# A layer kernel with its loops written out, each tile loaded a turn earlier, and a new list of steps

## The chip, the cores and the metric

The kernel runs on one core of a Trainium2 chip. The metric is the device time of one execution in microseconds. PE is the matmul engine, PEld its weight loads, DVE and ACT the vector and the scalar engine, POOL and SP the two others; SP issues all DMAs here.

## The reference

Four graph layers, each with a residual and a layer norm, over 128 graphs of 64 nodes and 512 features:

```
x = layernorm(x + hypergraph(x, adj, W1, W2))        # layer 0
x = layernorm(x + pairwise(x, adj, w, a))            # layer 1
h = relu(adj @ (x @ W1) + b1)                        # layer 2
h = relu(adj @ (h @ W2) + b2)
x = layernorm(x + adj @ (h @ W3) + b3)
q, k, v = split(x @ W_qkv)                           # layer 3, 8 heads of 64
attn = 0.33 softmax(q k^T / 8) + 0.33 adj + 0.33 exp(-adj)
x = layernorm(x + (attn @ v) @ W_out + b_out)
```

## The kernel before

Two graphs of 64 nodes make a tile of 128 rows; there are 64 tiles, worked on four at a time (tiles 0 to 3 of a turn), so 16 turns. The program has two halves, one after the other with a barrier between: `hypergraph_and_pairwise` does layers 0 and 1 and stores x2 to memory, `convolutions_and_attention` reads x2 and does layers 2 and 3.

In each half every engine goes through one hand-written list, ORDER, and does its own part of each entry: `g0.1` is step g0 of tile 1, and a `+` says that it belongs to the next turn (software pipelining). START holds the entries with `+` (turn 0), then a hardware loop (Fori) runs ORDER 15 times, and END holds the entries without `+`. In the loop, the values that a wait compares with are computed in registers at the head of each turn. The engines meet only through semaphores. SP has a loop of its own with the loads and the stores.

The steps of the second half, with their lines: `at` turns the adjacency blocks AB into AT (DVE, line 1024). `t0`, `t1`, `t2` multiply by the adjacency: 32 small matmuls of 64 x 64 (PE 1140), a cast of the result to Th (ACT 942) and the remainder Tl (DVE 1004). `g0`, `g1`, `g2` are projections of 12 matmuls of 128 x 512 (PE 1109); behind g0 and g1 DVE adds the bias (1032) and ACT does the relu (946). `b3` adds a bias to X (1035), `z3`, `rs3`, `x3` are residual and norm (DVE 1042, 1007 to 1011, POOL 864, DVE 1047), `xp` transposes (PE 1150), `v` and `qk` project (PE 1109; qk for a pair of tiles, 96 matmuls of 256 columns; its copies to QK on ACT 962 and DVE 1054), `s` makes scores (PE 1171, DVE 1058 to 1062), `sm` the softmax (ACT 966, DVE 1065 to 1073), `ta` transposes it (PE 1178, copies ACT 971 and DVE 1076), `av` multiplies by v (PE 1185, ACT 974, DVE 1004), `wo` projects, `z4`, `rs4`, `x4` are the last residual and norm (DVE 1084, POOL 864, DVE 1089), `cm` prepares masks (ACT 951, POOL 869 to 881). In the first half `tx`, `t2`, `t3` are small matmuls (PE 581), `y1`, `y2`, `y3` projections (PE 561).

Before, PE's part of the second list reads: ta.0 ta.1 av.0 s.2 s.3 av.1 wo.0 wo.1 ta.2 t0.0+ av.2 g0.0+ wo.2 ta.3 t0.1+ av.3 t1.0+ g0.1+ wo.3 t0.2+ t1.1+ ... xp.2+ qk.0+ xp.3+ v.2+ v.3+ s.0+ s.1+ qk.1+, and then the jump back.

X holds the residual of a tile until `z4`; SP loads the next tile into it behind `z4` (line 808), and `t0` waits for that load.

Of the kernel before, what the change touches and what calls it, by code (L numbers as in the profile page):

```python
# [44 lines left out]
def hypergraph_and_pairwise(nc, semaphores, x, adj, W1T, b1, gamma, beta, W2T, b2, w, wT, a, x2, slots, later):  # L45
# [9 lines left out]
    with ExitStack() as ctx:  # L55
# [162 lines left out]
        def _(pool):  # L218
# [60 lines left out]
            with pool.Fori(0, iters - 1) as it:  # L279
                steps(ORDER, it, pool.to_reg)  # L280
# [3 lines left out]
        def _(act):  # L284
# [80 lines left out]
            with act.Fori(0, iters - 1) as it:  # L365
                steps(ORDER, it, act.to_reg)
# [3 lines left out]
        def _(dve):  # L370
# [174 lines left out]
            with dve.Fori(0, iters - 1) as it:  # L545
                steps(ORDER, it, dve.to_reg)
# [3 lines left out]
        def _(pe):  # L550
# [122 lines left out]
            with pe.Fori(0, iters - 1) as it:  # L673
                steps(ORDER, it, pe.to_reg)
# [11 lines left out]
def convolutions_and_attention(nc, semaphores, x2, adj, mask_rows, mask_cols, E, AA, QK, slots, b1, b2, b3, Wqkv, bout, out):  # L686
# [9 lines left out]
    with ExitStack() as ctx:  # L696
# [23 lines left out]
        X = sb("X2", [P, CH, D])  # L720
        H = sb("H", [P, CH, D])
# [14 lines left out]

        def by_graph(W, c):
            return W[:, :, c * P:(c + 1) * P].rearrange("p k (g j) -> p k g j", g=2)
# [4 lines left out]
        blocks_in = sem("blocks_in")  # L743
# [6 lines left out]
        (at_ok, mc_ok, row_ok, mm_ok, bs_ok, exp_adj, bt3, cm2, cm_ok, b3_ok, bo_ok, z3, bn3, mv3,  # L750
         ve3, rs3, x3_ok, xp_ps, xph, xp_sb, v_ps, v_sb, s_ps, sbs_ok, max_ok, nb_ok, ex_ok, rec_ok, rla_ok, soft_ok, attn_ok,
         ta_psA, ta_psB, ta_sbA, ta_sbB, av_ps, avh, av_sb, wo_ps, z4, bn4, mv4, ve4, rs4, x4_ok) = map(sem, (
            "at_ok2 mc_ok row_ok mm_ok bs_ok exp_adj bt3 cm2 cm_ok b3_ok bo_ok z3 bn3_2 mv3_2 "
# [31 lines left out]
        def _(sp):  # L785
            def load_blocks(tile):

                for g in range(2):
                    for b in range(2):
                        for c in range(CH):  # L790
                            sp.dma_start(AB[g * C + b * C // 2:g * C + (b + 1) * C // 2, c, :].rearrange("p (a j) -> p a j", a=2),
                                         adj_b[g, b, :, bass.ds(tile + c, 1), :, :].rearrange("i t a j -> i (t a) j")).then_inc(blocks_in, 16)
# [14 lines left out]
            def load_x(c, tile):  # L807
                sp.dma_start(X[:, c, :], x2[bass.ds(tile, 1)].rearrange("a r d -> (a r) d")).then_inc(x_in[c], 16)
# [4 lines left out]
            load_blocks(0)  # L813
            for c in range(CH):
                load_x(c, c)
            load_masks(0)
            for k in range(KD):
                sp.wait_ge(split_lo, (4, 4, 6, 8)[k])
                sp.dma_start(raw_qkv[k], Wqkv[k * P:(k + 1) * P, :]).then_inc(load_in[k], 16)
            for i in range(2):  # L820
# [21 lines left out]
            sp.wait_ge(blocks_in, 16 * 4 * CH * iters)  # L842
# [5 lines left out]
        def _(pool):  # L848
# [48 lines left out]
            with pool.Fori(0, iters - 1) as it:  # L897
                steps(ORDER, it, pool.to_reg)
# [33 lines left out]
        def _(act):  # L932
            def steps(entries, it, reg):
# [3 lines left out]
                for step, c, ahead in entries:  # L937
# [9 lines left out]
                    if step == "cm":  # L947
                        act.wait_ge(masks_in, loaded[ahead])
                        if entries is not START:
                            act.wait_ge(attn_ok, at[ahead - 1][CH - 1])  # L950
# [31 lines left out]
            with act.Fori(0, iters - 1) as it:  # L982
                steps(ORDER, it, act.to_reg)
# [259 lines left out]
```

## Time and profile before

| | |
|---|---|
| median of 3 runs | 2844.67 us (2843.2 to 2847.39) |
| the profiled execution | 2846.66 us, span 2844.9 us |
| busy: PE | 2659.1 us, 93% |
| busy: PEld | 2197.8 us, 77% |
| busy: DVE | 1820.5 us, 64% |
| busy: ACT | 879.0 us, 31% |
| busy: POOL | 474.9 us, 17% |
| mean granted clock of TensorE | 0.978 |

The first half ends near 1158 us, the second half's weights are ready near 1194 us, its loop runs from 1279 to 2811 us. A busy share is a mean over stages. "Issue" in the profile is time in which an engine waited for nothing that the profile shows. Busy times of matmuls overlap, so the distance from one start to the next says more of their cost than their durations.

### The profile page before, as it was taken

The numbers are of one execution on the slowest core, as the hardware profiler recorded it, in microseconds if no ns is written. First come the engines' busy times: TensorE is split into PE (matmuls) and PEld (weight loads), VectorE is DVE, ScalarE is ACT, GpSimd is POOL, SyncE is SP. The second block draws the span as 40 slices with busy tenths as digits, with TensorE's granted clock in tenths as the row PEclk, the third lists the DMA queues.
The fourth block names the chain that finished last, engine by engine and source line by source line (L and its number), as shares of the span: only waits on it lengthen the run. The fifth ranks groups of instructions, "written<-read, shape, count | busy, mean of one in ns | idle before, by whom it ended". The sixth has DMA issues, their size and how long they took to land.

```text
span 2844.9 us, 73879 instructions
## 1 busy us (share of the span) xinstructions
PE 2659.1 (93%) x30296; PEld 2197.8 (77%) x30296; DVE 1820.5 (64%) x3754; ACT 879.0 (31%) x2397; POOL 474.9 (17%) x749
## 2 busy tenths in 40 slices
PE   3999999999999999299999999999999999999998
PEld 2778778777777778287788788788788778878877
DVE  3778887788878887446545655654654655565565
ACT  2222322222222222233332332333333333233233
POOL 0222222222222222010110111011011011101101
PEclk9999999999999999699999999999999999999999
DMA  5111111111111110201101100100110110110010
GB/s 181 28 38 36 35 35 35 38 36 36 38 36 40 42 35 19 97 6 33 37 8 33 38 13 28 36 25 19 33 31 13 33 38 10 29 38 17 26 32 16
DMA packets 130004, 99.41 MB, mean 35 GB/s; under 512 B 89104, under 2 KB 91152, under 8 KB 129808
## 3 DMA queue, kind: packets, MB, share of 16 engines
q1 hardware_dynamic: 129808, 96.30, 11.4%
q8 instruction: 184, 3.01, 0.5%
q14 instruction: 12, 0.10, 0.0%
HBM read 62.68 MB, written 33.55 MB: 34 GB/s over the span
## 4 chain that ended last, share of the span: by engine, by line
PE 52%; DVE 4%; issue 2%; ACT 1%; SPq 1%; DMA 0%; DVEq 0%; POOLq 0%
PE qs L1109 43%; PE qs L1140 4%; PE qs L1171 1%; PE qs L1178 1%; DVE T2l L1004 1%; PE qs L1150 1%; PE qs L1185 1%; ACT T2h L942 1%; DVE sm L1007 0%; DVE Z L1084 0%; DVE E L1069 0%; DVE E L1073 0%; DMA QK<-in_L_Wqkv 0%; DVE sm L1060 0%; DVE E L1058 0%
## 5 line engine op out<-in xcount | busy, mean ns | idle before, releaser
L1109 PE MATMUL qs<-hi,T2h 128*128 128x512 f32 x1024 | 422.0, 412 | 24.5 <-DVE T2l L1004 24.1
L1109 PE MATMUL qs<-hi,T2l 128*128 128x512 f32 x1024 | 406.9, 397 | 0.0
L1109 PE MATMUL qs<-lo,T2h 128*128 128x512 f32 x1024 | 406.5, 397 | 0.0
L1004 DVE TENSOR_TENSOR T2l<-qs,T2h 128x512 fp32r<-128x512 f32 x320 | 212.9, 687 | 183.1 <-ACT T2h L942 110.9
L864 POOL TENSOR_TENSOR sm<-sm,mhalf 128x1 f32<-128x1 f32 x128 | 86.2, 673 | 1370.6 <-DVE sm L1011 1370.6
L1109 PE MATMUL qs<-T2h,WQh 128*128 128x256 f32 x1024 | 291.2, 284 | 0.0
L1109 PE MATMUL qs<-T2h,WQl 128*128 128x256 f32 x1024 | 288.2, 281 | 0.0
L1109 PE MATMUL qs<-T2l,WQh 128*128 128x256 f32 x1024 | 288.1, 281 | 0.0
L1109 PEld LDWEIGHTS qs<-hi,T2h 128*128 128x128 f32 x1024 | 194.6, 190 | 78.5 <-DVE T2l L1004 34.8
L1109 PEld LDWEIGHTS qs<-hi,T2l 128*128 128x128 f32 x1024 | 194.5, 190 | 46.1
L1109 PEld LDWEIGHTS qs<-lo,T2h 128*128 128x128 f32 x1024 | 195.1, 190 | 39.8
L561 PE MATMUL ps<-W2h,Th 128*128 128x512 f32 x512 | 204.3, 399 | 5.1 <-issue 4.5
L561 PE MATMUL ps<-W1h,Th 128*128 128x512 f32 x512 | 206.8, 404 | 0.6 <-DVE Tl L411 0.6
L561 PE MATMUL ps<-W1l,Th 128*128 128x512 f32 x512 | 201.4, 393 | 0.0
L561 PE MATMUL ps<-W1h,Tl 128*128 128x512 f32 x512 | 201.2, 393 | 0.0
L561 PE MATMUL ps<-W2h,Tl 128*128 128x512 f32 x512 | 199.7, 390 | 0.0
L561 PE MATMUL ps<-W2l,Th 128*128 128x512 f32 x512 | 199.5, 390 | 0.0
L946 ACT ACTIVATE H<-H 128x512 f32<-128x512 f32 x128 | 81.2, 634 | 368.5 <-DVE H L1032 368.5
L1109 PEld LDWEIGHTS qs<-T2h,WQh 128*128 128x128 f32 x1024 | 192.7, 188 | 1.1
L1109 PEld LDWEIGHTS qs<-T2l,WQh 128*128 128x128 f32 x1024 | 192.8, 188 | 0.0
L1109 PEld LDWEIGHTS qs<-T2h,WQl 128*128 128x128 f32 x1024 | 192.7, 188 | 0.0
L966 ACT ACTIVATE E<-E,sm 128x64 f32<-128x64 f32 x512 | 172.0, 340 | 32.1 <-DVE sm L1062 31.6
(175 smaller groups left out, 5319.3 us busy)
## 6 DMA issues: line engine op xcount, KB each, us to landing
X<-in_x SPq DMA_DIRECT2D x64, 256.0 KB, 6.5
x<-R SPq DMA_DIRECT2D x64, 256.0 KB, 2.0
X<-x SPq DMA_DIRECT2D x64, 256.0 KB, 2.9
out<-Z SPq DMA_DIRECT2D x64, 256.0 KB, 3.1
AB<-in_adj SPq DMA_DIRECT2D x512, 8.0 KB, 1.6
A<-in_adj SPq DMA_DIRECT2D x128, 32.0 KB, 2.2
An<-in_adj SPq DMA_DIRECT2D x16, 128.0 KB, 2.3
WB<-in_adj SPq DMA_DIRECT2D x32, 64.0 KB, 7.3
```

Of the source, the lines that this page charges most:

```text
L561: mm = pe.matmul(out, lhsT, rhs, start=start and i == 0, stop=i == len(terms) - 1)
L864: return pool.tensor_tensor(col(c, RS), col(c, VE), mhalf[:, :], ALU.pow)
L942: act.copy(by_graph(Th, c), halves(c)).then_inc(th[i], 1)
L946: act.activation(H[:, c, :], H[:, c, :], ACT.Relu).then_inc(g_sb[i], 1)
L966: last = act.activation(EH(c)[:, h, :], EH(c)[:, h, :], ACT.Exp, bias=col(c, NB + h), scale=SCALE, accum_out=col(c, SUM + h))
L1004: return dve.tensor_tensor(lo, ps, hi.bitcast(F32), ALU.subtract)
L1109: mm = pe.matmul(out, lhsT, rhs, start=i == 0, stop=i == len(terms) - 1)
L1140: mm = pe.matmul(half[q, k * C:(k + 1) * C], rows[g, k * P + q.start:k * P + q.stop], AT[g, c, :], start=True, stop=True)
L1150: mm = pe.transpose(psA[c][:, k * P:(k + 1) * P], X[:, c, k * P:(k + 1) * P], ident[:, :])
L1171: mm = pe.matmul(ps[c][y * C:(y + 1) * C, x, (n_ * 2 + g) * C:(n_ * 2 + g + 1) * C], QK[x * C:(x + 1) * C, m, rows_g], QK[x * C:(x + 1) * ...
L1178: mm = pe.transpose(ps[c][:, x, n_ * P:(n_ + 1) * P], E[:, c, x * 2 + n_, :], ident[:, :])
L1185: mm = pe.matmul(ps[c][x * C:(x + 1) * C, g, (2 * n_ + y) * C:(2 * n_ + y + 1) * C], H[rows_g, c, h * DHEAD:(h + 1) * DHEAD], AA[rows_g, c ...
```

## The change

In both halves the loops of PE, DVE, ACT and POOL become Python loops, so that the 15 turns stand written out in a row, with numbers in place of registers. SP keeps its loops. In the second half:

- Tile c of the next turn is loaded into a buffer of its own, `xn(c)`: XN for tiles 0 and 1, an unused part of AA for 2 and 3. The load waits for the two readers of that buffer, `t0.c` (PE) and `b3.c` (DVE), and no longer for `z4.c`. `t0` reads xn(c); it now waits for `z4` of the tile before itself, since both use the same PSUM banks. `b3` reads xn(c) and writes X.
- AB is turned into AT in two instructions, for tiles 0 and 1 (`at.0`) and 2 and 3 (`at.1`), each with its own semaphores; the blocks are loaded per pair.
- The stores come behind all loads of SP's turn.
- ORDER is new. PE's part reads: s.1 qk.1 ta.0 ta.1 s.2 av.0 av.1 s.3 wo.0 wo.1 ta.2 t0.0+ av.2 g0.0+ t0.1+ wo.2 ta.3 t1.0+ av.3 g0.1+ wo.3 t0.2+ t1.1+ g1.0+ g1.1+ t2.0+ t0.3+ ... g2.2+ t2.3+ v.1+ xp.2+ g2.3+ qk.0+ xp.3+ v.2+ v.3+ s.0+.

```diff
+        XN = sb("XN", [P, 2, D])
+        def xn(c):
+            return XN[:, c, :] if c < 2 else AA[:, 3 - c, HEADS // 2:HEADS, :].rearrange("p h j -> p (h j)")
...
         ORDER = order(
-            "ta.0 ta.1 av.0 s.2 s.3 av.1 wo.0 z4.0 sm.2 wo.1 rs4.0 x4.0 at.0+ ta.2 t0.0+ av.2 b3.0+ z4.1 sm.3 rs4.1 g0.0+ "
-            "wo.2 x4.1 ta.3 t0.1+ av.3 z4.2 b3.1+ t1.0+ rs4.2 g0.1+ wo.3 x4.2 t0.2+ t1.1+ z4.3 rs4.3 x4.3 g1.0+ b3.2+ g1.1+ "
-            "t0.3+ t2.0+ g0.2+ g2.0+ z3.0+ rs3.0+ b3.3+ t1.2+ t2.1+ g0.3+ x3.0+ g1.2+ xp.0+ g2.1+ z3.1+ rs3.1+ bo.0+ t1.3+ "
-            "t2.2+ x3.1+ v.0+ g1.3+ xp.1+ g2.2+ bo.1+ t2.3+ z3.2+ v.1+ rs3.2+ x3.2+ g2.3+ z3.3+ rs3.3+ x3.3+ xp.2+ bo.2+ "
-            "qk.0+ cm.0+ xp.3+ bo.3+ v.2+ v.3+ s.0+ s.1+ sm.0+ sm.1+ qk.1+")
+            "s.1 sm.0 bo.2 bo.3 sm.1 qk.1 ta.0 ta.1 s.2 av.0 av.1 rs4.0 s.3 sm.2 z4.0 wo.0 at.0+ wo.1 ta.2 rs4.1 x4.0 t0.0+ "
+            "av.2 z4.1 sm.3 g0.0+ rs4.2 rs4.3 b3.0+ x4.1 t0.1+ wo.2 ta.3 at.1+ t1.0+ av.3 z4.2 g0.1+ x4.2 wo.3 z4.3 t0.2+ "
+            "t1.1+ g1.0+ x4.3 g1.1+ b3.1+ t2.0+ rs3.0+ b3.2+ t0.3+ b3.3+ g0.2+ g2.0+ z3.0+ t1.2+ t2.1+ x3.0+ rs3.1+ g0.3+ "
+            "g1.2+ xp.0+ g2.1+ z3.1+ t2.2+ t1.3+ v.0+ x3.1+ g1.3+ xp.1+ rs3.2+ g2.2+ z3.2+ t2.3+ x3.2+ v.1+ xp.2+ bo.0+ z3.3+ "
+            "g2.3+ x3.3+ qk.0+ bo.1+ rs3.3+ xp.3+ v.2+ cm.0+ v.3+ s.0+")
...
@@ SP, second half @@
             with sp.Fori(0, iters - 1) as it:
                 t0 = sp.snap(it * CH)
-                sp.wait_ge(at_ok, sp.snap(it + 1))
-                load_blocks(t0 + CH)
+                for p in range(2):
+                    for c in (2 * p, 2 * p + 1):
+                        sp.wait_ge(t_ps[0], sp.snap(t0 + (c + 1)))
+                        sp.wait_ge(b3_ok, sp.snap(t0 + (c + 1)))
+                        load_x(c, t0 + (CH + c))
+                    sp.wait_ge(at_ok[p], sp.snap(it + 1))
+                    load_blocks(t0 + CH, p)
                 sp.wait_ge(cm_ok, sp.snap(it + 1))
                 load_masks(t0 + CH)
                 for c in range(CH):
-                    sp.wait_ge(z4, sp.snap(t0 + (c + 1)))
-                    load_x(c, t0 + (CH + c))
-                    if c:
-                        store(c - 1, t0)
-                store(CH - 1, t0)
+                    store(c, t0)
...
@@ PE, second half; the same in the other engines and in the first half @@
             steps(START, -1, number)
-            with pe.Fori(0, iters - 1) as it:
-                steps(ORDER, it, pe.to_reg)
+            for it in range(iters - 1):
+                steps(ORDER, it, number)
             steps(END, iters - 1, number)
...
@@ DVE @@
-                        dve.transpose(AT[:, :, :].rearrange("p c i -> p (c i)"), AB[:, :, :].rearrange("p c i -> p (c i)")).then_inc(at_ok, 1)
+                        pair_c = slice(2 * c, 2 * c + 2)
+                        alone(blocks_in[c], blocks[ahead])
+                        if each[ahead] > 1:
+                            dve.wait_ge(t_ps[2], (each[ahead] - 2) * CH + 2 * c + 2)
+                        dve.transpose(AT[:, pair_c, :].rearrange("p c i -> p (c i)"), AB[:, pair_c, :].rearrange("p c i -> p (c i)"))\
+                            .then_inc(at_ok[c], 1)
...
-                        dve.wait_ge(t_ps[0], n[c])
-                        dve.tensor_tensor(X[:, c, :], X[:, c, :], b3_all[:, :], ALU.add).then_inc(b3_ok, 1)
+                        dve.wait_ge(x_in[c], x_loaded[ahead])
+                        dve.tensor_tensor(X[:, c, :], xn(c), b3_all[:, :], ALU.add).then_inc(b3_ok, 1)
...
@@ PE, step t0 @@
-                            alone(at_ok, each[ahead])
+                            alone(at_ok[c // 2], each[ahead])
                             pe.wait_ge(x_in[c], x_loaded[ahead])
+                            if n[c] > CH:
+                                pe.wait_ge(z4, n[c] - CH)
```

## Rows read from the trace of the kernel before

**Rows 1.** The page: code fetches (packets, MB, share); groups (busy, mean ns, idle before).

```profile
q8 instruction: 184, 3.01, 0.5%
...
L1004 DVE TENSOR_TENSOR T2l<-qs,T2h 128x512 fp32r<-128x512 f32 x320 | 212.9, 687 | 183.1 <-ACT T2h L942 110.9
...
L966 ACT ACTIVATE E<-E,sm 128x64 f32<-128x64 f32 x512 | 172.0, 340 | 32.1 <-DVE sm L1062 31.6
```

**Rows 2.** Waits of PE: for whom, us in total, times, longest.

```profile
PE qs L1178 <- issue: 30.1, 14, 2.4
...
PE ps L561 <- issue: 4.5, 14, 0.4
```

**Rows 3.** Lines 1195 and 673, PE's loops: duration ns min/median/max, first and last start.

```profile
L1195 PEldq COMPARE_BRANCH  x15: 79/3619/3799, 1375.5 to 2809.3; - x15
...
L673 PEldq COMPARE_BRANCH  x15: 76/208/245, 169.7 to 1116.3; - x15
```

**Rows 4.** Timeline of PE around a jump: start us, length us, engine, line, idle before.

```profile
1787.78 0.28 PE L1109 MATMUL qs<-T2h,WQl 128*128 128x256 f32 x1
...
1790.28 1.72 PE L1178 MATMUL qs<-ident,E 128*128 128x128 f32 x8 [2.23 <-issue]
...
1795.02 0.51 PE L1109 MATMUL qs<-hi,T2h 128*128 128x512 f32 x1
...
1801.89 0.66 PE L1178 MATMUL qs<-ident,E 128*128 128x128 f32 x4 [0.66 <-DVE E L1073]
1802.74 0.69 PE L1140 MATMUL qs<-AT,X 64*64 64x64 f32 x32 [0.20 <-issue]
...
1804.86 0.50 PE L1109 MATMUL qs<-hi,T2h 128*128 128x512 f32 x1 [0.95 <-DVE T2l L1004]
...
1818.98 0.69 PE L1140 MATMUL qs<-AT,X 64*64 64x64 f32 x32
```

**Rows 5.** The same view where the loop is left.

```profile
2811.18 0.28 PE L1109 MATMUL qs<-T2h,WQl 128*128 128x256 f32 x1
2811.30 1.03 PE L1178 MATMUL qs<-ident,E 128*128 128x128 f32 x8
...
2815.06 0.50 PE L1109 MATMUL qs<-hi,T2h 128*128 128x512 f32 x1
```

**Rows 6.** Stretches: busy us (count) of PE, PEld, DVE, ACT, POOL; clock, DMA.

```profile
1587.00:1689.00 102.00, 96.59 (x1103) 81.57 (x1102) 57.41 (x113) 33.86 (x106) 11.76 (x14) 1.00 0.10 27
1790.60:1794.00 3.40, 3.40 (x76) 2.94 (x77) 1.10 (x3) 1.33 (x3) 0.00 (x0) 0.50 0.00 0
```

**Rows 7.** Chain that ended last: start us, us; the matmuls of qk.1.

```profile
1776.47 11.59 PE qs L1109 x96
```

**Rows 8.** Timeline of PE, first half, first passes: y2.2 three times, a wait.

```profile
101.64 0.49 PE L561 MATMUL ps<-W2h,Th 128*128 128x512 f32 x1
...
147.57 0.45 PE L581 MATMUL ps<-CU,R 64*64 64x64 f32 x12 [0.66 <-issue]
...
170.43 0.49 PE L561 MATMUL ps<-W2h,Th 128*128 128x512 f32 x1 [0.36 <-issue]
...
238.03 0.49 PE L561 MATMUL ps<-W2h,Th 128*128 128x512 f32 x1 [0.32 <-issue]
```

**Rows 9.** Timeline of DVE, with a cast of ACT, in the stretch of rows 4.

```profile
1793.13 0.59 ACT L974 CAST T2h<-qs 128x512 fp32r<-128x512 f32 x1 [1.15 <-PE qs L1185]
...
1794.36 0.68 DVE L1058 TENSOR_TENSOR E<-qs,BS 128x512 f32<-128x512 f32 x1
...
1795.90 0.69 DVE L1058 TENSOR_TENSOR E<-qs,BS 128x512 f32<-128x512 f32 x1
...
1798.10 0.69 DVE L1084 TENSOR_TENSOR Z<-qs,X 128x512 f32<-128x512 f32 x1
...
1799.98 0.19 DVE L1065 RECIPROCAL sm<-sm 128x8 f32<-128x8 f32 x1
...
1802.20 0.43 DVE L1024 STREAM_TRANSPOSE AT<-AB 128x256 f32<-128x256 f32 x1
```

More of the change, by code:

```diff
@@ L364, in _ @@
             steps(START, -1, number)
-            with act.Fori(0, iters - 1) as it:
-                steps(ORDER, it, act.to_reg)
+            for it in range(iters - 1):
+                steps(ORDER, it, number)
             steps(END, iters - 1, number)
@@ L544, in _ @@
             steps(START, -1, number)
-            with dve.Fori(0, iters - 1) as it:
-                steps(ORDER, it, dve.to_reg)
+            for it in range(iters - 1):
+                steps(ORDER, it, number)
             steps(END, iters - 1, number)
@@ L672, in _ @@
             steps(START, -1, number)
-            with pe.Fori(0, iters - 1) as it:
-                steps(ORDER, it, pe.to_reg)
+            for it in range(iters - 1):
+                steps(ORDER, it, number)
             steps(END, iters - 1, number)
@@ L742, in convolutions_and_attention @@
         load_in = [sem(f"load2_in{i}") for i in range(KD)]
-        blocks_in = sem("blocks_in")
+        blocks_in = [sem(f"blocks_in{p}") for p in range(2)]
+        at_ok = [sem(f"at_ok2_{p}") for p in range(2)]
         masks_in = sem("masks_in")
@@ L812, in _ @@
             sp.wait_ge(consts_ok, 3)
-            load_blocks(0)
-            for c in range(CH):
+            for p in range(2):
+                load_blocks(0, p)
+            for c in range(2):
                 load_x(c, c)
@@ L819, in _ @@
                 sp.dma_start(raw_qkv[k], Wqkv[k * P:(k + 1) * P, :]).then_inc(load_in[k], 16)
+                if k == 2:
+                    load_x(2, 2)
+            sp.wait_ge(split_lo, len(pieces) + KD - 1)
+            load_x(3, 3)
             for i in range(2):
@@ L827, in _ @@
                 t0 = sp.snap(it * CH)
-                sp.wait_ge(at_ok, sp.snap(it + 1))
-                load_blocks(t0 + CH)
+                for p in range(2):
+                    for c in (2 * p, 2 * p + 1):
+                        sp.wait_ge(t_ps[0], sp.snap(t0 + (c + 1)))
[3 more added lines that the diff above has]
+                    load_blocks(t0 + CH, p)
                 sp.wait_ge(cm_ok, sp.snap(it + 1))
@@ L841, in _ @@
                 sp.wait_ge(x_in[c], 16 * iters)
-            sp.wait_ge(blocks_in, 16 * 4 * CH * iters)
+            for p in range(2):
+                sp.wait_ge(blocks_in[p], 16 * 2 * CH * iters)
             sp.wait_ge(masks_in, 16 * MASK_LOADS * iters)
@@ L896, in _ @@
             steps(START, -1, number)
-            with pool.Fori(0, iters - 1) as it:
-                steps(ORDER, it, pool.to_reg)
+            for it in range(iters - 1):
+                steps(ORDER, it, number)
             steps(END, iters - 1, number)
@@ L948, in steps @@
                         act.wait_ge(masks_in, loaded[ahead])
-                        if entries is not START:
-                            act.wait_ge(attn_ok, at[ahead - 1][CH - 1])
+                        if each[ahead] > 1:
+                            act.wait_ge(attn_ok, (each[ahead] - 1) * CH)
                         act.copy(MM[:, :, :, :], mrow[:, :, :, :]).then_inc(row_ok, 1)
@@ L981, in _ @@
             steps(START, -1, number)
-            with act.Fori(0, iters - 1) as it:
-                steps(ORDER, it, act.to_reg)
+            for it in range(iters - 1):
+                steps(ORDER, it, number)
             steps(END, iters - 1, number)
@@ L1016, in steps @@
                 stored = [[reg(it * 32 + (32 * a + 16 * (r + 1))) for r in range(2)] for a in (0, 1)]
-                blocks = [reg(it * (64 * CH) + 64 * CH * (a + 1)) for a in (0, 1)]
+                x_loaded = [reg(it * 16 + 16 * (a + 1)) for a in (0, 1)]
+                blocks = [reg(it * (32 * CH) + 32 * CH * (a + 1)) for a in (0, 1)]
                 for step, c, ahead in entries:
@@ L1092, in _ @@
             steps(START, -1, number)
-            with dve.Fori(0, iters - 1) as it:
-                steps(ORDER, it, dve.to_reg)
+            for it in range(iters - 1):
+                steps(ORDER, it, number)
             steps(END, iters - 1, number)
@@ L1194, in _ @@
             steps(START, -1, number)
-            with pe.Fori(0, iters - 1) as it:
-                steps(ORDER, it, pe.to_reg)
+            for it in range(iters - 1):
+                steps(ORDER, it, number)
             steps(END, iters - 1, number)
```

19 lines of the change are left out of this document (7 added, 12 removed).

## The prediction, made before the changed kernel ran

> **What bounds the kernel now.** I read the profile from the outside in. First the page: PE is busy 93% of the span (the table above), and code is fetched in 184 packets of 3.01 MB in all [rows 1]. So the reader should look only for time in which PE waits, and ask who ends it. The list of PE's waits gives it [rows 2]: 30.1 us in 14 waits "for issue" ahead of line 1178, and only 4.5 us in 14 waits for issue at line 561. Line 1178 is the first PE line of a turn in the second half, line 561 that of the first half, and 14 is the number of jumps back. Third, the branch lines [rows 3]: the taken jump of PE's second loop takes 3619 ns in the median, that of the first loop 208 ns. Both jumps are the same instruction, so what differs is what it jumps into: the long body of the second half has to be brought in again, the body of the first does not.
>
> Fourth, one turn of the second half in order of time [rows 4]. The last matmul of `qk.1` starts at 1787.78, `ta.0` at 1790.28: 2.50 us. Where no jump lies between them, at the end of the loop, the same two starts are 0.12 us apart [rows 5]. So a jump costs 2.38 us here, of which the profile shows 2.23 as idle. Then `ta.0` to `wo.0` takes 4.74 us in the loop and 3.76 us after it [rows 4, 5], for the same matmuls: the idle time drops the granted clock to its lower level (1.2 GHz) in the stretch behind this jump [rows 6]; not behind every jump, for 1587 to 1689 has 1.00 throughout. Further on PE waits 0.66 us for `ta.2` (softmax of tile 2) and 0.95 us for `g0.0` [rows 4]. Ten turns lie between 1790.28 and 2811.30, 102.1 us each [rows 4, 5].
>
> **The change, part by part.**
>
> *1. Jump of the second half, removed 14 times.* The idle part: 30.1 us [rows 2], scaled by 2.38 / 2.23 to starts, 32 us. The slower stretch behind it: 4.74 - 3.76 = 0.98 us, times 14, 14 us. Together -46 us. The register arithmetic that goes with it lies inside the same gap. SP keeps its loop. For DVE, ACT and POOL the jump is not on the path: PE starts `ta.0` later than their own list is ready, and it will still be PE that comes last behind `qk.1`, 11.6 us of matmuls [rows 7].
>
> The Trainium skill ("Advanced Engine Details and Errata", Control Flow Timing) gives a compare-and-branch about 108 ns; by that figure 28 jumps are worth 3 us and, with the list, the forecast would be about 2824. The trace does not agree for either loop, 208 and 3619 ns [rows 3], and leaves this case no chance. The same page (ISA Cache) gives TensorE 128 KB in lines of 16 KB and the other engines 32 KB, and "Vector Engine (DVE) Microarchitecture Reference" (The three layers) 64 bytes an instruction; by these the second body of PE does not fit and the first does, which agrees with the two durations, and it speaks against unrolling the first half, which is part 2.
>
> *2. Jump of the first half, removed 14 times, and its code fetched anew.* Gain: 4.5 us idle [rows 2], about 6 us by starts. Cost: until now only the first pass had to be fetched. It took 170.43 - 101.64 = 68.8 us against 238.03 - 170.43 = 67.6 us, and PE stood idle for issue 0.66 us in the middle of a dense run of small matmuls (`t2.1`) [rows 8]. Written out, every pass is a first pass. Bounds: nothing (the long 128x512 matmuls leave time to fetch, and no wait for issue of size stands inside the second half's body, which is fetched each turn) and 15 x 1.2 = 18 us. Whether a boundary of fetched code falls into the dense run changes from turn to turn; I take a third, 6 us. Net 0, between -6 and +12.
>
> *3. The new list between `qk.1` and `t0.2`, walked.* Units: a cast on ACT 0.59 [rows 9], a remainder on DVE 0.69, eight exponentials of one tile 8 x 0.34 = 2.7 [rows 1]; 96 matmuls of 256 columns take 11.6 [rows 7], so a projection (12 of 512 columns) 2.8 to 2.9; a step of 32 small ones 0.5 (3.76 for four of them, eight transposes and small waits, [rows 5]). Time runs from the last start of `qk.1`, no jump. PE does `ta.0 ta.1 s.2 av.0 av.1 s.3`, the same matmuls as in [rows 5], and is free at 3.5 to 3.9. But on DVE `s.2` now stands ahead of the remainder of `av.0`: scores of tile 2 are there at 2.2, they hold DVE 1.54 us (1794.36 to 1795.90 for one tile [rows 9]), then 0.69 for the remainder: `wo.0` starts at 4.5. That is a new wait of 0.6 to 1.0 us. `wo.0` and `wo.1` end at 10.1. ACT's exponentials of tile 2 begin at 3.9 behind the `av.1` cast and take 2.7; DVE's sm.2 takes 1.9 (1799.98 to the start of `ta.2`, 1801.89 [rows 4, 9]) and now comes before `z4.0`: done at 8.6, so `ta.2` no longer waits (-0.66). `z4.0` with its statistics takes 1.9 to 2.0 (before, from 1798.10, ending behind the first operation of sm.2 [rows 9]), to 10.55; the half-size transposition, some 0.25, comes next, and `t0.0` starts at 10.9, 0.3 after `ta.2`. Cast 0.59 and remainder 0.69 follow: `g0.0` at 12.95, a wait of about 1.0, as before. From there g0.0 2.88, `t0.1` 0.5 (now ahead of `wo.2`, which only the early load allows), wo.2 2.8, `ta.3` 0.5, `t1.0` 0.5, 0.4 for the AA copy of tile 3, which stands on DVE behind `x4.1` and `t0.1`, `av.3` 0.5, g0.1 2.88, wo.3 2.8: `t0.2` at 26.7, 26.6 after `ta.0`. Before it is 1818.98 - 1790.28 = 28.7, and 27.7 without the slow stretch that part 1 has counted. Gain 1.1 us.
>
> *4. The rest of the list.* `xp.2` now follows `g2.2` after only `t2.3` and `v.1` (3.3 us), while z3.2, statistics, POOL's power and x3.2 need about 3.6: a new wait of 0.3. The `cm.0` step comes one projection later; its result reaches DVE's s.0 about 1.4 us late, hidden by `qk.1` (11.6 us, of which scores, exponentials and softmax of tiles 0 and 1 use some 11). If that cover is gone, `ta.0` waits up to 1 us. Net of parts 3 and 4: -0.8 a turn, -12 us; bounds -30 (all new waits vanish) and +15 (each is a microsecond longer).
>
> *5. Early loads and the pair-wise transposition.* `t0.0` (1802.74) follows the AT transposition, which starts at 1802.20 [rows 4, 9], and not the load. So the second buffer is worth nothing itself, only through the list. New waits: on SP x(c) waits for `t0.c` and b3.c, with blocks, masks and stores queued behind; all are needed most of a turn later, except the stores, which need x4 and find SP idle there. On PE `t0.c` waits for z4 of the tile before, done at 9.3 in the walk against 10.9. DVE has one more transposition instruction, and b3 keeps its size. Cost 0, hidden by DVE's idle time.
>
> *6. Start and end.* The list is cut elsewhere: `s.1` and `qk.1` go from the start to the end, equal work. The end has no t0 and g0 between the tiles, and loses the wait for sm.2: -3 us. Two of the turns before are some 2 us longer than the others by a double slow stretch behind the jump: -3 us.
>
> Sum: -46 + 0 - 12 - 3 - 3 = -64 us. The profiled execution took 2846.7 (its span 2844.9 and 1.8 around it), 2.0 above the median of the runs; a difference carries over: 2844.7 - 64 = 2781.
>
> **The rivals.**
> (a) *The list gives nothing*: only the jump is gone, 2845 - 46 = 2799. For it: two waits leave and three come. Against: the longest (`ta.2`) surely goes. Chance 0.17.
> (b) *The new wait at `wo.0` drops the clock* in each turn, as the jump did: +0.98 x 15 = 15, 2796. For it: it follows small matmuls, as in [rows 6]. Against: before, 0.66 and 0.95 us of waiting within 4 us left the clock at 1.00 in the turn from 1587 [rows 4, 6]. Chance 0.12.
> (c) *Waits of the list vanish* since engines run closer than my walk: 2845 - 46 - 30 - 6 = 2763. Chance 0.13.
> (d) *Slower: PE starves for code.* Written out, all 30 turns fetch. It decides from (64 + 6) / 30 = 2.3 us of stall a turn; at 2.5 a turn +75 against -64 gives 2856. The one measured first pass shows 1.2 in all, and the second half fetches each turn without it. (The cache sizes of the page named in part 1 are the rule that speaks for this case.) Chance 0.04. That unrolling costs just what it saves (within 0.2%): 0.03.
> (e) *The change does not do what it says*: loads still land late since x waits for b3. b3.0 to b3.3 stand in the first half of a turn, the use a turn later: excluded.
>
> **How the numbers follow.** Forecast 2781 with chance 0.51, its own range 2770 to 2792. The range reaches to (a), (b) and (c) with the bound of part 2 on top: 2760 to 2808. Faster than 0.2% (about what this kernel's runs can tell from no change): 0.51 + 0.17 + 0.12 + 0.13 = 0.93; same 0.03; slower 0.04.
>
> **What the changed profile would show.** Right: no wait for issue at the turn's first matmul; `ta.0` 0.1 us behind `qk.1`; granted clock 1.00 through the loop; turns of 98.2 us; first-half turns of 67 to 68.5 us with short waits for issue at line 581; code packets up by half or more; at `wo.0` a wait for line 1004 of 0.6 to 1.0. Wrong: waits for issue in the small matmuls of both halves (d), turns of 99 or more with the clock at 1.00 (a), lower clock behind `wo.0` (b).

## The result, and the profile after

| | before | after |
|---|---|---|
| median, us | 2844.13 (2843.2 to 2847.39) | 2779.22 (2776.96 to 2780.73) |
| ratio | | 0.977, 95% interval 0.975 to 0.979 |
| span of the profiled execution | 2844.9 | 2775.1 |
| first starts of the second half's turns | 1278.57 to 2811.30 | 1265.58 to 2733.19 |
| mean turn of the second half | 102.2 | 97.8 |
| mean turn of the first half | 67.7 | 67.6 |

The forecast was 2781, the range 2760 to 2808. By medians the change is worth 64.9 us; the two profiled spans differ by 69.8, since the one of before lies 2.5 us above its median and the one of after 2.3 us below. In the traces the loop of the second half gives 65.1 of it, the first half's loop 0.3, the end 3.8, the start 0.9 (the start differs by up to 3 us between traces of the same code), and the stretch between the two loops takes 0.3 back. A turn of the second half is counted from `ta.0` before and from `s.1` after, the first entry of each list. One further execution of a kernel below, `loop_first`, took 3290.38 us at a mean granted clock of 0.75, and its ratio leaves that one out.

The page of after: span, and the code fetches that answer to [rows 1].

```profile
span 2775.1 us, 73243 instructions
...
q8 instruction: 240, 3.93, 0.6%
```

The waits of PE in after (for whom, us in total, times, longest), against [rows 2]. The 30.1 us for issue are gone, and 14 waits at line 561 with them; what is left for issue is 1.3 us in the first half and 0.2 in the second. The line for T2l, 29.9 us in 35 waits, is two waits in each turn: the one at `wo.0` is new (0.8 us each), the one at `g0.0` stood in the old list too (0.95 in [rows 4], 0.85 now).

```profile
PE qs L1124 <- DVE T2l L1016: 29.9, 35, 1.4
...
PE ps L581 <- issue: 1.3, 2, 0.9
```

The windows view over the whole second half of after, in the columns of [rows 6]: the granted clock is 1.00 all through.

```profile
1199.00:2758.90 1559.90, 1529.58 (x17566) 1299.12 (x17565) 932.07 (x1802) 535.67 (x1685) 162.70 (x221) 1.00 0.09 26
```

The timeline of after where [rows 4] stood, PE and the operations of DVE that set its waits (start us, length us, engine, line, operation, idle before). `ta.0` follows `qk.1` after 0.12 us. `wo.0` (1672.89) waits for the remainders of `av.0` and `av.1` (1672.15), which stand behind the scores of tile 2 (1670.63). `g0.0` (1681.32) waits for the remainder of `t0.0` (1680.57). `t0.2` starts 26.7 us after `ta.0`.

```profile
1668.62 0.28 PE L1124 MATMUL qs<-T2h,WQl 128*128 128x256 f32 x1
1668.74 1.04 PE L1195 MATMUL qs<-ident,E 128*128 128x128 f32 x8
...
1670.63 0.69 DVE L1073 TENSOR_TENSOR E<-qs,BS 128x512 f32<-128x512 f32 x1 [0.33 <-PE qs L1188]
...
1672.15 1.28 DVE L1016 TENSOR_TENSOR T2l<-qs,T2h 128x512 fp32r<-128x512 f32 x2
...
1672.89 0.50 PE L1124 MATMUL qs<-hi,T2h 128*128 128x512 f32 x1 [0.79 <-DVE T2l L1016]
...
1676.85 0.68 DVE L1099 TENSOR_TENSOR Z<-qs,X 128x512 f32<-128x512 f32 x1
...
1678.57 0.60 PE L1195 MATMUL qs<-ident,E 128*128 128x128 f32 x4
...
1678.79 0.31 DVE L1038 STREAM_TRANSPOSE AT<-AB 128x128 f32<-128x128 f32 x1
...
1679.20 0.69 PE L1157 MATMUL qs<-AT,XN 64*64 64x64 f32 x32
...
1680.57 1.29 DVE L1016 TENSOR_TENSOR T2l<-qs,T2h 128x512 fp32r<-128x512 f32 x2 [0.47 <-ACT T2h L954]
...
1681.32 0.50 PE L1124 MATMUL qs<-hi,T2h 128*128 128x512 f32 x1 [0.85 <-DVE T2l L1016]
...
1695.42 0.69 PE L1157 MATMUL qs<-AT,AA 64*64 64x64 f32 x32
```

### The profile page after: what moved, and what is told of

Same layout as the page of the kernel before. It is cut to its first block, busy times and chain, and to the rows that moved or that the text cites. A ratio compares the mean times of both kernels' runs of the same rounds, so it can differ in the third digit from the quotient of the medians.

```text
span 2775.1 us, 73243 instructions
## 1 busy us (share of the span) xinstructions
PE 2636.8 (95%) x30296; PEld 2185.2 (79%) x30296; DVE 1836.8 (66%) x3770; ACT 871.9 (31%) x2397; POOL 451.2 (16%) x749
## 4 chain that ended last, share of the span: by engine, by line
PE 54%; DVE 2%; SPq 1%; ACT 1%; issue 0%; DMA 0%; DVEq 0%; POOLq 0%; POOL 0%
PE qs L1124 47%; PE qs L1157 4%; PE qs L1188 1%; PE qs L1167 1%; PE qs L1195 1%; DVE T2l L1016 1%; PE qs L1202 0%; DVE E L1073 0%; DVE sm L1075 0%; ACT T2h L954 0%; DMA QK<-in_L_Wqkv 0%; SPq L796 0%; SPq L803 0%; DVE sm L1077 0%; SPq L809 0%
## 5 line engine op out<-in xcount | busy, mean ns | idle before, releaser
L1124 PE MATMUL qs<-hi,T2h 128*128 128x512 f32 x1024 | 421.4, 411 | 29.9 <-DVE T2l L1016 29.9
L876 POOL TENSOR_TENSOR sm<-sm,mhalf 128x1 f32<-128x1 f32 x128 | 70.6, 552 | 1232.9 <-DVE sm L1023 1232.9
```

What stands on the lines that cost most here:

```text
L876: return pool.tensor_tensor(col(c, RS), col(c, VE), mhalf[:, :], ALU.pow)
L1124: mm = pe.matmul(out, lhsT, rhs, start=i == 0, stop=i == len(terms) - 1)
```

## The experiments

The median of before was 2842.78 beside `loop_first` and 2844.18 beside the other timed kernels. Starts given as means "after `ta.0`" are means over the turns of each kernel's trace.

### The loops alone: u_both and u_first

```diff
 kernel before, list and loads unchanged
-            with pe.Fori(0, iters - 1) as it:
-                steps(ORDER, it, pe.to_reg)
+            for it in range(iters - 1):
+                steps(ORDER, it, number)
 the same for DVE, ACT, POOL; u_both: in both halves, u_first: in the first half alone
```

> The kernel before with both sets of loops written out and nothing else: old list, one buffer, one transposition. Theory (the jump of the second half is the bulk): 14 jumps of 2.4 us with 1 us of slower start behind each are gone, 2844 - 46 = 2798 (2790 to 2806); turns of the second half 98.7 to 99.1 us instead of 102.1, all alike. Rival (the jump only hides other waits, which come back: softmax of tile 2, remainder of t0.0): 2815 or more, turns over 100 us. Rival (the list of the change is what pays): within 5 us of 2844.

Measured: 2792.65 (2791.74 to 2793.25), ratio 0.982 (0.980 to 0.984): 51.5 us less. Turns are 98.8 us, all alike. Its waits of PE have no line for issue at the turn's start, and the wait for the softmax of tile 2 is there, a little shorter than in before (12.6 us in 16):

```profile
PE qs L1178 <- DVE E L1073: 10.2, 17, 0.8
```

> The kernel before with the loops of the first half alone written out. Theory: 0.4 us a turn gained at the jump, about as much given back in turns in which the code of the small matmuls arrives late; 2844 within 4 us. Rival (nothing is given back): 2837, turns of 67.0. Rival (each pass costs what the first pass cost, 1.2 us more): 2855.

Measured: 2846.65, ratio 1.0007 (0.9998 to 1.0017). So 51.5 belongs to the second half, and the new list with the early loads adds 2792.65 - 2779.22 = 13.4.

### The list without the written-out turns: list_loop

```diff
 kernel after
-            for it in range(iters - 1):
-                steps(ORDER, it, number)
+            with pe.Fori(0, iters - 1) as it:
+                steps(ORDER, it, pe.to_reg)
 the same for DVE, ACT, POOL, in both halves; waits on earlier turns put back in register form
```

> The changed kernel with the loops of PE, DVE, ACT and POOL kept as loops in both halves: new list, early loads, pair-wise transposition alone. The jump now stands between s.0 and s.1. Theory (parts add up): PE waits some 3 us at the jump since only s.0 is queued ahead of it, but qk.1 comes soon after, so no slow start: 2826 (2816 to 2834), turns near 101. Rival (list and loops are tied, the list gives nothing with a jump in it): 2840 to 2845. Rival (the list is most of the gain): 2800 or less.

Measured: 2867.92 (2862.91 to 2868.9), ratio 1.008 (1.006 to 1.010). A miss by 42 us: without the written-out turns the new list and its early loads make the kernel slower than before. Its waits of PE, the jump at `s.1` in the turn at 1680, and the stretch behind it (windows, columns as [rows 6]):

```profile
PE qs L1188 <- issue: 60.7, 15, 4.6
```

```profile
1680.59 1.13 PE L1188 MATMUL qs<-QK 64*64 64x64 f32 x32 [4.03 <-issue]
...
1695.60 1.04 PE L1195 MATMUL qs<-ident,E 128*128 128x128 f32 x8
```

```profile
1680.20:1686.80 6.60, 6.21 (x56) 6.12 (x57) 4.90 (x12) 5.53 (x32) 0.18 (x1) 0.50 0.17 37
```

The jump itself takes as long as before, but less of it is covered. The branch lines of one turn (engine's queue, duration ns, start), first of before, then of this kernel:

```profile
L1195 PEldq COMPARE_BRANCH  x1: 3623/3623/3623, 1785.9 to 1785.9; - x1
```

```profile
L1212 PEldq COMPARE_BRANCH  x1: 3294/3294/3294, 1676.2 to 1676.2; - x1
```

In before the sequencer reaches the jump at 1785.9, while the matmuls of `qk.1` queued ahead of it run on until 1788.06 [rows 4]: 2.2 of the 3.6 us are covered. The new list jumps behind `s.0`, 32 small matmuls that start at 1675.87 and are over at 1676.56; some 0.4 us is covered and PE waits 4.0 us. Behind it stands `qk.1`, which is 1.7 us longer than in after (13.2 against 11.5 from its start to `ta.0`, means over the 14 turns behind a jump and over all turns of after); in all 14 the granted clock falls to 0.50 there. The expectation had the clock stay up, since `qk.1` comes soon. So writing the turns out is worth 51.5 us under the old list and 2867.92 - 2779.22 = 88.7 under the new one, with the early loads.

### Is the slow stretch behind the jump the clock? pause

```diff
 u_both
 DVE, step qk of the second pair, last bank: two more copies of QK in series, each waited for
+                                for z in pz:
+                                    dve.tensor_copy(QK[:, 2 * b:2 * b + 2, :], by_pair(bank(c, b))).then_inc(z, 1)
+                                    dve.wait_ge(z, each[ahead])
 PE, step ta of tile 0
+                            pe.wait_ge(consts_ok, 3)
+                            pe.wait_ge(qk_sb[3], pair[0][1])
```

> The kernel before with all loops written out and, ahead of ta.0, a pause of PE of about the length of the jump's: DVE makes the last QK copy of a turn three times, and ta.0 waits for the third (some 2.1 us behind qk.1). No code is fetched anew. Theory clock (the idle time alone lowers the granted clock, and that made the start of a turn slow): clock 0.5 behind most pauses, ta.0 to wo.0 4.6 to 4.9 us, 2793 + 48 = 2841. Theory code (the slow start was the second piece of code arriving late): ta.0 to wo.0 stays at 3.8 to 3.9 us, 2793 + 32 = 2825.

Measured: 2844.89, 52.2 more than u_both, ratio to before 1.0002 (0.9993 to 1.0012). From `qk.1` to `ta.0` it is 2.44 us longer than in u_both, with all code in its place; there are 16 such pauses (the first is ahead of the first full turn), and behind 13 of them the granted clock is at its lower level for 3.4 us: 16 x 2.44 + 13 x 1.0 = 52. Its waits of PE, and the windows behind one pause:

```profile
PE qs L1186 <- issue: 36.5, 16, 2.3
```

```profile
1691.05:1694.40 3.35, 3.35 (x108) 3.07 (x99) 2.42 (x5) 0.83 (x2) 0.00 (x0) 0.50 0.02 5
```

Where the clock stays up (three turns of 101.13 us), the turn is 1.0 us shorter than most others (102.1). That is the price of one drop. It doesn't explain all of the slow stretch: `ta.0` to `wo.0` takes 4.41 us here in the mean, 5.07 in before (the 14 turns behind a jump) and 3.68 in u_both. A part of the rest is a second wait for issue, which u_both, with the same list and no jump, doesn't have; code that arrives late a second time would explain it. The timeline of PE in before behind the jump of 1586, a turn whose clock stayed at 1.00, and the windows there and behind the next jump:

```profile
1586.05 1.09 PE L1178 MATMUL qs<-ident,E 128*128 128x128 f32 x8 [2.12 <-issue]
...
1588.87 0.27 PE L1185 MATMUL qs<-AA,H 64*64 64x64 f32 x1 [0.87 <-issue]
...
1591.15 0.50 PE L1109 MATMUL qs<-hi,T2h 128*128 128x512 f32 x1
```

```profile
1586.10:1589.50 3.40, 2.18 (x51) 1.72 (x55) 0.85 (x2) 1.07 (x3) 0.00 (x0) 1.00 0.02 5
1688.20:1691.60 3.40, 3.40 (x61) 2.98 (x65) 0.85 (x2) 1.20 (x3) 0.00 (x0) 0.50 0.00 0
```

31 of the 32 small matmuls of `av.0` run, the last waits 0.87 us; in all four turns of before that have this wait it is the last one. From `ta.0` to `wo.0` 5.10 us pass here at the full clock, more than the 4.74 at half clock behind the jump of [rows 4]. Of the 14 turns behind a jump, all three at the full clock have this wait (0.93, 0.87, 0.40), and one of the 11 with the lower clock (0.54). That slower matmuls leave the fetch its time is a reading of this, not shown: in u_first seven of the twelve turns with the lower clock have the wait too.

### What makes the jump cost 3.6 us: short_second and the split kernels

```diff
 short_second: kernel before, second half
-                for k in range(KD):
+                for k in range(KD // 2):
-                    terms += three(...)
+                    terms += three(...)[:1]
 split_all: kernel before, first half, y1, y2 and y3 (split_y1: y1 alone)
+                if halved:
+                    for q in (slice(0, D // 2), slice(D // 2, D)):
+                        mm = products(out[:, q], [(l, r[:, q]) for l, r in terms])
 split_two: as split_y1, with two of the three products
+                    terms = [t for i, t in enumerate(terms) if i % 3 < 2]
```

> The kernel before, loops kept, but every projection matmul of the first half (y1, y2, y3) made as two of 256 columns: the same products, and PE's loop body of the first half grows from 1638 to some 2120 instructions, about as long as that of the second half. Theory (a jump costs what has to be fetched again, and that depends on the length of the body): PE's jump in the first half goes from 208 ns to 3.3 to 3.8 us, with waits for issue at line 561 of 1 us or more in 14 turns. Rival (the long jump belongs to something else in the second half): 208 ns as before.

> The kernel before, loops kept; in the first half only projection y1 (line 561) is written as two products of 256 columns, so the loop body of PE grows from about 1640 to about 1830 instructions, still short of the 2120 of the kernel in which y1, y2 and y3 were split and whose jump took 3.6 us. Theory that the length of the body decides, with a step between 1830 and 2120: the taken jump of PE's first loop stays near 208 ns, no wait for issue over 0.5 us at the turn's first matmul, granted clock 1.00 in the first half's loop. Rival that splitting a product itself makes the jump slow (other code, more instructions in flight): 3.6 us again, with about 3.5 us idle behind each jump. Rival that the cost grows with the length in proportion: something near 1.5 us. The time of the kernel is of no matter here: its first half has more matmuls than before.

> The kernel before, both loops kept. In the first half y1 is written as two products of 256 columns, and of its three products of parts only two are computed (so its result is not the reference's): the traced body of PE's first loop has about 1664 instructions, between the 1600 of before (208 ns) and the 1792 of the kernel with y1 split in full (3.3 to 3.9 us). Rival that splitting a product itself makes the jump slow: 3.6 us again. Theory that the length decides, with the step at a whole number of pieces of code: 208 ns if the step lies between 1664 and 1792, which I hold for likelier (0.65) than a step between 1600 and 1664 (3.6 us, which would leave the rival standing). A value between, near 1 us, would speak for a cost that grows with the length.

> The kernel before, both loops kept. In the second half every projection (g, v, wo and qk) computes only the product of the two high parts and only half of the contraction: 72 matmuls a turn instead of 432 (so its result is not the reference's). The traced body of PE's second loop falls from 2248 to about 1528 instructions, below the 1600 of the first loop. Theory that the length of the body decides: the taken jump at line 1195 falls from 3.6 us to about 0.2 us, no wait for issue of more than 0.5 us at the turn's first matmul. Rival that something else in the second half makes the jump slow (its place in the list, its registers, the DMAs beside it): 3.3 to 3.8 us as before. The turn is much shorter in any case, and DVE may become the bound; its length tells nothing.

Each was timed once, for its branch lines alone. short_second leaves out two of the three products and half of the contraction of every projection, split_two one of the three products of y1. The lengths named ahead of split_all and split_y1 (1638, 1830, 2120) are some 40 above what the traces hold; the table below counts the traces. Measured, by the branch lines of PE (duration ns min/median/max, first and last start), in the order split_all, split_y1, split_two, short_second:

```profile
L677 PEldq COMPARE_BRANCH  x15: 79/3599/3938, 170.4 to 1220.7; - x15
```

```profile
L677 PEldq COMPARE_BRANCH  x15: 76/3592/3928, 168.8 to 1203.2; - x15
```

```profile
L678 PEldq COMPARE_BRANCH  x15: 76/3483/3777, 163.9 to 1156.4; - x15
```

```profile
L1195 PEldq COMPARE_BRANCH  x15: 76/208/225, 1314.0 to 2396.2; - x15
```

| kernel, loop | PE's instructions in the traced body | taken jump, ns |
|---|---|---|
| short_second, second half | 1528 | 208 |
| before, first half | 1599 | 208 |
| split_two, first half | 1663 | 3483 |
| split_y1, first half | 1791 | 3592 |
| split_all, first half | about 2080 | 3599 |
| before, second half | 2247 | 3619 |

short_second settles the loop in question: the same loop at the same line, with two thirds of the body, jumps in 208 ns. The price has no middle value, so it doesn't grow with the length; there is a step. Two of the four expectations missed: for split_y1 the theory said 208 ns, and for split_two I had held a step between 1664 and 1792 for likelier (0.65). The step lies between 1599 and 1663, if length is all that splitting changes. No unsplit body of 1663 was tried, so this place of the step is the weaker half of the claim: the rival that splitting itself makes a jump slow stands for the three split kernels. What unsplit bodies alone show is that the price changes somewhere between 1599 and 2247.

The Trainium skill ("Runtime: NRT & Kernel Launch", Instruction fetch mechanics) says that a taken branch whose target lies outside the current window of two pages forces a fetch and a stall. The four long bodies agree, with 3.5 to 3.6 us; the bodies of 1528 and 1599 don't: at the page's 256 instructions a block they are longer than two blocks and jump in 208 ns. It gives TensorE room for 2048 instructions; by that figure the bodies of 1663 and 1791 would jump in 208 ns, and the traces show 3483 and 3592. The measurement decides: the longest body seen here with the short jump is some 450 traced instructions below that size.

### What the early loads are worth: late_load

```diff
 kernel after, SP
-                        sp.wait_ge(t_ps[0], sp.snap(t0 + (c + 1)))
-                        sp.wait_ge(b3_ok, sp.snap(t0 + (c + 1)))
-                        load_x(c, t0 + (CH + c))
...
                 for c in range(CH):
+                    sp.wait_ge(z4, sp.snap(t0 + (c + 1)))
+                    load_x(c, t0 + (CH + c))
```

> The changed kernel with the loads of x put back behind z4 of the same tile, everything else as changed (buffers, list, loops written out). Theory (early loading matters only through the list, but there it does): the load for tile 0 is issued at z4.0 and takes 2.7 us, so t0.0 starts some 1.9 us later than now; nothing is late at tiles 1 to 3; 2779 + 28 = 2807 (2798 to 2815). Rival (the load is hidden anyway, since PE waits for DVE at that place): 2779 within 4.

Measured: 2818.59, ratio 0.991 (0.989 to 0.993), 39.4 more than after. Turns of 100.6 us. The direction was right, the size too small: I had priced the wait at `t0.0` and not the one at `t0.1`. The edit also puts the stores back between the loads, as before. The windows line below, behind the timeline, is one of five turns in which the granted clock falls behind `t0.0`. Its waits of PE, and PE's timeline in one turn:

```profile
PE qs L1157 <- DMA XN<-x: 33.4, 25, 1.6
```

```profile
1691.09 0.60 PE L1195 MATMUL qs<-ident,E 128*128 128x128 f32 x4
1692.95 0.69 PE L1157 MATMUL qs<-AT,XN 64*64 64x64 f32 x32 [1.26 <-DMA XN<-x]
...
1699.60 0.69 PE L1157 MATMUL qs<-AT,XN 64*64 64x64 f32 x32
```

```profile
1695.60:1698.90 3.30, 3.30 (x9) 2.54 (x8) 2.95 (x9) 1.82 (x12) 0.55 (x1) 0.50 0.39 107
```

`t0.0` starts 1.86 us after `ta.2` (0.63 in after), and `t0.1` 18.44 after `ta.0` instead of 15.63: in the means 1.4 us are lost up to `t0.0` and 1.4 more up to `t0.1`. The falls of the clock matter little, for turns with and without one take 100.3 to 101.1 us. This kernel is slower than u_both, which has the old list and late loads: without the early loads the new list costs 26 us more than the old one.

### Is there room on DVE between qk.1 and g0.0? av0_first and t0_first

```diff
 av0_first: kernel after, in DVE's list alone the remainder of av.0 ahead of s.2
+            DVE_ORDER.insert(DVE_ORDER.index(("s", 2, 0)), DVE_ORDER.pop(DVE_ORDER.index(("av", 0, 0))))
 t0_first: kernel after, at.0+ moved from behind wo.0 to behind ta.1, in PE's list t0.0+ ahead of ta.2
+            i, j = PE_ORDER.index(("ta", 2, 0)), PE_ORDER.index(("t0", 0, 1))
+            PE_ORDER.insert(i, PE_ORDER.pop(j))
```

> The changed kernel, but DVE alone does the remainder of av.0 ahead of the scores of tile 2. Theory (the wait at wo.0 is the order on DVE, but DVE is busy without a break from there to t0.0, so what wo.0 gains ta.2 or t0.0 loses): the wait at wo.0 falls from 1.0 to about 0.5 us, a new one of up to 0.5 us comes at ta.2 or t0.0, 2779 within 5. Rival (the wait at wo.0 is a loss of PE's own and nothing is behind it): 2779 - 8 = 2771.

Measured: 2822.88, 43.7 more than after, ratio 0.993 (0.991 to 0.995). A miss, for the theory and for the rival. PE's timeline in one turn, DVE's in the same turn, then the windows before and behind `t0.0`:

```profile
1684.93 0.50 PE L1127 MATMUL qs<-hi,T2h 128*128 128x512 f32 x1 [0.27 <-DVE T2l L1016]
...
1691.15 0.65 PE L1198 MATMUL qs<-ident,E 128*128 128x128 f32 x4 [0.36 <-DVE E L1091]
1693.36 0.69 PE L1160 MATMUL qs<-AT,XN 64*64 64x64 f32 x32 [1.56 <-DVE AT L1041]
```

```profile
1684.18 0.69 DVE L1016 TENSOR_TENSOR T2l<-qs,T2h 128x512 fp32r<-128x512 f32 x1 [1.33 <-ACT T2h L986]
1684.79 0.68 DVE L1076 TENSOR_TENSOR E<-qs,BS 128x512 f32<-128x512 f32 x1
...
1691.01 0.68 DVE L1102 TENSOR_TENSOR Z<-qs,X 128x512 f32<-128x512 f32 x1
```

```profile
1684.00:1691.00 7.00, 6.52 (x56) 4.95 (x56) 5.86 (x12) 3.40 (x18) 0.00 (x0) 1.00 0.01 2
1694.30:1701.00 6.70, 5.93 (x31) 4.12 (x29) 4.73 (x10) 3.64 (x18) 0.55 (x1) 0.50 0.10 39
```

The wait at `wo.0` falls from 0.79 to 0.27, as it should. But DVE does its list in order, and the remainder of `av.0` isn't ready: DVE stands idle for 1.33 us until ACT's cast is there, where in after it does the scores of tile 2. Those start 3.5 us after `ta.0` (1684.79 - 1681.30) instead of 1.9 (1670.63 - 1668.74), so the exponentials and `sm.2` come later too, and `z4.0`, which stands behind them on DVE, starts 9.7 us after `ta.0` instead of 8.1 (1676.85 - 1668.74). `t0.0` waits 1.56 for the transposition behind it. In 7 of the 15 turns the granted clock is then at 0.50 for 6.8 us, in one for 3.4: those turns are 101.7 to 102.1 and 100.6 us, the others 99.3 to 99.4. So about half of the loss is the later `z4.0` (1.5 us in each turn) and most of the rest the clock.

> The changed kernel with two moves: at.0 (the transposition of the next turn's first pair) goes ahead of s.2 on DVE, and PE alone does t0.0 before ta.2. Theory (the wait of 1.1 us at g0.0 is the chain z4.0, transposition, t0.0, cast, remainder, and t0.0 could start 0.6 us earlier): 0.6 us a turn less, 2779 - 10 = 2769 (2763 to 2775). Rival (DVE has no time to spare in this stretch, so g0.0 starts when it did): 2779 within 3.

Measured: 2782.93, ratio 0.979 (0.977 to 0.980), 3.7 more than after: a miss, and the rival was right. PE's timeline in one turn:

```profile
1680.82 0.69 PE L1161 MATMUL qs<-AT,XN 64*64 64x64 f32 x32
1681.45 0.66 PE L1199 MATMUL qs<-ident,E 128*128 128x128 f32 x4
1682.71 0.69 PE L1206 MATMUL qs<-AA,H 64*64 64x64 f32 x32 [0.61 <-DVE AA L1091]
```

`t0.0` is 0.5 us earlier, but `ta.2`, its copies and `av.2` are later, and `g0.0` starts 12.83 after `ta.0` instead of 12.65. The two waits of some 1 us that are left in a turn are for DVE. t0_first only moved one of them, av0_first made DVE wait itself; that no other order of this stretch would do better isn't shown.

### The first half with its loop, the second as changed: loop_first

```diff
 kernel after, first half alone
-            for it in range(iters - 1):
-                steps(ORDER, it, number)
+            with pe.Fori(0, iters - 1) as it:
+                steps(ORDER, it, pe.to_reg)
```

> The changed kernel with hardware loops kept in the first half alone; second half as changed. Theory (in the first half the saved jumps and the code fetched anew cancel, and the halves are independent but for the barrier between them): 2779.5, between 2776 and 2783, with the second half's turns at 98 us as in the changed kernel. Rival that the code written out in the first half matters for the second (where the second half's first turns find their code): the start of the second half longer by 1 to 3 us, 2781 to 2783. Rival that the first half alone is better with loops: 2774 or less.

Measured: 2774.97, ratio 0.976 (0.975 to 0.977). That is 1.0 below the range expected and 1.0 above the rival's. By the two ratios and their intervals it isn't told apart from after; the other five executions (2774.74 to 2776.54) all lie below the four of after (2776.96 to 2780.73), with before beside them 1.4 lower, so a gain of some 2 or 3 us by the loop isn't excluded. The loop of its first half takes 1015.3 us from first to last start against 1014.7, the second half's 1467.3 against 1467.6; the 2 us by which its span is shorter lie ahead of the first turn, where no loop has run (the stretch between the loops is 1.7 shorter, the end 1.5 longer). With u_first this says twice that writing out the first half gives nothing. What it costs in code is plain from the pages, first u_first, then this kernel:

```profile
q8 instruction: 271, 4.44, 0.6%
```

```profile
q8 instruction: 153, 2.51, 0.4%
```

Against before [rows 1], 87 packets more; against after, 87 less. With the second half written out and the new list there are 31 fewer than in before (153 against 184); list_loop has 184 and u_both 240, as after, so the list has no part in it.

## Why the prediction was right, point by point

The mechanism held: the jump of the second half is most of the gain, the first half gives nothing, the list adds about 1 us a turn. That the sum of 64 meets the 64.9 so closely is in part luck: the jump and the list were put too low and the end too high.

**1, the jump of the second half: right in kind, 5 us short.** The term was 46, and 3 more stood in part 6 for the double slow stretches, which are the same effect; u_both measures 51.5. The idle part held: `ta.0` now follows `qk.1` after 0.12 us, and the means of the traces give 32 us for it. The term that was mis-sized is the slower stretch behind it, 0.98 a turn: in the means `ta.0` to `wo.0` shrinks from 5.07 to 3.68, by 1.39, which is 19.5 us in 14 turns. I took one turn for all, and one cause for two: pause puts the clock alone at 1.0 where it falls, and the turn of 1586 shows a second wait for issue at the full clock. So the sentence that no such wait of size stands inside the second half's body was a misreading: there are four, up to 0.93 us. That the length of the body decides held (short_second); where the bound lies no trace had shown, and split_two and split_y1 have the long jump from 1663 traced instructions on, with split matmuls.

**2, the first half: right.** Net 0 was forecast; u_first gives 1.0007 and loop_first no difference outside the intervals. The first half's turns in after are 67.4 to 67.7, one 68.1 and one 68.7, with a stall in the small matmuls (0.92 us idle, 1.2 in all) like that of the first pass [rows 8]. Both terms were too large: a turn without a stall gained 0.1 us (67.6 to 67.5), not 0.4, and the stall came in one turn of 14 behind the first, not in a third of them. It didn't change from turn to turn as I had thought: in all seven kernels with the first half written out it stands in the tenth turn, 754 to 757 us into the span, with 0.38 to 0.92 us of idle time.

**3, the new list to `t0.2`: right.** Forecast walk against the mean of after, from `ta.0`: `wo.0` 4.4 / 4.16, `ta.2` 10.0 / 9.87, `t0.0` 10.8 / 10.49, `g0.0` 12.8 / 12.65, `t0.2` 26.6 / 26.77. The gain on u_both (27.90) is 1.13, forecast 1.1. The new wait at `wo.0` is 1.0 in the mean by starts, the upper end of 0.6 to 1.0 (0.8 as idle time).

**4, the rest of the list: the wait wasn't there.** The 0.3 at `xp.2` and the 0.4 in front of `av.3` (measured 0.16) were walked too late. Net of parts 3 and 4 the turn is 98.84 - 97.84 = 1.0 shorter, forecast 0.8: 15 us where 12 stood.

**5, the early loads: the term 0 held, the sentence on them was too narrow.** That they are worth nothing except through the list agrees with the runs. How much hangs on that was not worked out: without them the list costs 39.4 us more, half of it at `t0.0`, whose load then comes later than the transposition, and half at `t0.1`, which stands ahead of `wo.2`.

**6, start and end: right by chance.** The end is 3.8 us shorter in the trace of after, where the term had 3 for the list. But u_first, whose second half is that of before, ends as fast as u_both: from the last `ta.0` on it is 33.6 us in before, 30.4 in u_first, 30.3 in u_both and 29.7 in after. The difference to before is the granted clock, 0.80 in that stretch of its trace and 0.99 and 0.98 in the two others; against those two the list itself is worth some 0.5 us there, with the clock at 0.90 in after. The windows from the last `ta.0` to the end, before, u_first, u_both:

```profile
2811.30:2844.90 33.60, 22.50 (x258) 16.95 (x256) 19.83 (x43) 9.30 (x40) 2.25 (x4) 0.80 0.08 32
```

```profile
2811.60:2841.90 30.30, 18.30 (x258) 13.72 (x255) 19.86 (x43) 9.26 (x40) 2.27 (x4) 0.99 0.09 36
```

```profile
2759.40:2789.60 30.20, 18.25 (x258) 13.74 (x256) 19.76 (x43) 9.26 (x40) 2.25 (x4) 0.98 0.09 36
```

**The rivals.** (a), the list gives nothing, fell: 13.4 us. (b), the wait at `wo.0` drops the clock, fell here: behind 0.8 us of waiting the clock stayed at 1.00 in every turn. Its mechanism is real: av0_first has it at `t0.0`, behind 1.56 us of waiting, in 8 turns of 15, and late_load, behind 1.3 to 1.4 us, in 5. (c) fell: the waits at `wo.0` and `g0.0` are there. (d) fell: 1.5 us for issue in all. The forecast that code packets rise by half missed, 184 to 240: the first half adds 87, nearly half of 184, and the second half's went down.

**What the prediction didn't see** is that the parts don't add. It priced the jump where it stood, behind `qk.1`, which covers 2.2 us of it. The new list puts the turn's edge between `s.0` and `s.1`, where a jump costs 5.9 us a turn (88.7 / 15) instead of 3.4 (51.5 / 15). With all parts made together nothing of this shows.

## What to carry to other kernels

Read the branch lines of a loop before unrolling it: if the taken jump is 208 ns there was nothing to gain here, if it is 3.6 us, ask how much matmul work stands queued ahead of it and whether the body can be made short enough. Price each part of a change beside the others: here a list alone would have been thrown away as 1% slower, though it is worth 13 us once the turns are written out and the loads are early. Where an engine has two short waits left in a stretch, find the engine behind them, and before moving a step ahead on it ask when that step's input is ready: an engine that goes through its list in order stands idle for it. Two reorderings that each shortened one wait lost 4 and 44 us. And before a gain at the end of a trace is put down to the code, look at the granted clock there.

## What the runs showed of the hardware that was not expected

- The price of a taken jump on PE is a step: 208 ns up to 1599 traced instructions in the body, 3619 ns at 2247; 3483 ns already at 1663, in a body with split matmuls.
- Code written out costs PE almost nothing even in the small matmuls: in 30 turns of after two waits for issue at line 581, 1.3 us in all, and 0.2 in the second half. late_load, av0_first and t0_first have one more in `s.3` of one turn, 1.7, 1.2 and 1.0 us, and av0_first a further one of 1.0 at a `t0.0`; what brings these stays open.
- Behind a jump PE can wait twice: waits for issue of 2.12 us at the jump and of 0.87 us again 2.8 us later, at the full clock.
- One fall of the granted clock to 0.50 costs 1.0 us behind a pause of 2.3 us in front of small matmuls, and 1.7 us in the mean behind 4.0 to 4.6 us of waiting in front of `qk.1`. Whether it falls differs from turn to turn (13 of 16 pauses, 14 of 14 in list_loop, 8 of 15 turns in av0_first, 5 of 15 in late_load); what decides that stays open.
